# Score tiles moved into the projection, token lists from numbered rows, and 46 unread products on PE

## The reference

```python
# attention: 16 heads of 16, Q, K, V = norm(x) @ Wq, Wk, Wv
scores = jnp.einsum('bqhd,bkhd->bhqk', Q, K) / math.sqrt(HEAD_DIM)
alpha = jax.nn.softmax(scores, axis=-1)
alpha = jnp.where(causal, alpha, 0)             # masked after the softmax
Y = jnp.einsum('bhqk,bkhd->bqhd', alpha, V)
# experts: 8 experts, the best 2 of each of 4096 rows, hidden size 1024
h = jax.nn.gelu(flat_x @ w_fc[e], approximate=False)
out = out + combine[:, e:e + 1] * (h @ w_proj[e])
# together
x = x + _layernorm(attention(_layernorm(x)))
x = x + _layernorm(experts(_layernorm(x)))
```

## Time and profile before

| | us |
|---|---|
| median of 3 runs | 1625.13 (1625.03 to 1625.83) |
| profiled execution | 1626.82 |
| its span | 1625.1 |
| PE busy | 1455.0 (90%) |
| DVE busy | 1026.3 (63%) |
| ACT busy | 771.8 (47%) |
| POOL busy | 612.1 (38%) |
| mean granted clock of TensorE | 0.946 of 2.4 GHz |

### The profile page before, as it was taken

The page is one execution under the profiler, slowest core; times in us unless marked ns, Lnnn a source line. Parts: engine busy times, 40 slices in busy tenths (PEclk is TensorE's granted clock), DMA queues, the critical chain, the costliest instruction groups (busy, mean ns, idle before and its releaser), DMA issues.

```text
span 1625.1 us, 31177 instructions
## 1 busy us (share of the span) xinstructions
PE 1455.0 (90%) x9750; PEld 836.1 (51%) x9751; DVE 1026.3 (63%) x1770; ACT 771.8 (47%) x1650; POOL 612.1 (38%) x711
## 2 busy tenths in 40 slices
PE   5988999999999899989999986389999999999990
PEld 3551233333333233323333243289999999999980
DVE  4769777777888788878888977723323233233324
ACT  2330577777777677767777785211111111111114
POOL 5332334543444334533444432123333333333332
PEclk9995899999999999999999998589999999999995
DMA  3569122022220222022213153262222222222229
GB/s 113 172 164 276 40 40 40 10 31 40 40 40 8 35 40 40 15 27 40 40 23 70 53 182 142 45 183 34 39 33 38 39 33 39 34 37 39 32 30 210
DMA packets 87629, 105.07 MB, mean 65 GB/s; under 512 B 11648, under 2 KB 70912, under 8 KB 87520
## 3 DMA queue, kind: packets, MB, share of 16 engines
q1 hardware_dynamic: 69664, 80.80, 21.5%
q0 software_dynamic: 17856, 22.89, 8.9%
HBM read 64.70 MB, written 38.96 MB: 64 GB/s over the span
## 4 chain that ended last, share of the span: by engine, by line
PE 61%; DVE 15%; issue 13%; ACT 4%; POOL 3%; DMA 2%; DVEq 1%; SPq 0%; POOLq 0%; ACTq 0%
PE ps L1153 16%; PE ps L1163 15%; PE ps L1008 10%; DVE negmax L1443 9%; PE ps L980 8%; PE ps L1094 8%; ACT wfc L868 2%; POOL x L668 2%; PE ps L973 2%; PE ps L1081 1%; DVE x L1348 1%; PE ps L1142 1%; ACT wfc L911 1%; DVE wfc L1454 1%; DMA arena<-in_L_ffn_w_proj 1%
## 5 line engine op out<-in xcount | busy, mean ns | idle before, releaser
L1443 DVE TENSOR_REDUCE negmax<-ps 128x1 f32<-128x1024 f32 x512 | 605.9, 1216 | 123.8 <-PE ps L1094 121.3
L868 ACT ACTIVATE wfc<-ps 128x512 f32<-128x512 f32 x768 | 436.6, 595 | 171.2 <-PE ps L980 162.7
L889 ACT ACTIVATE yx<-ps 128x512 f32<-128x512 f32 x142 | 84.8, 597 | 440.6 <-PE ps L1153 440.6
L1153 PE MATMUL ps<-yx 128*128 128x128 f32 x2272 | 270.3, 278 | 4.1 <-DMA arena<-in_L_ffn_w_proj 3.4
L1153 PEld LDWEIGHTS ps<-yx 128*128 128x128 f32 x2272 | 269.7, 195 | 8.3 <-DMA arena<-in_L_ffn_w_proj 3.6
L1163 PE MATMUL ps<-arena,yx 128*128 x1136 | 256.8, 379 | 0.0
L731 POOL TENSOR_TENSOR wfc<-wfc,causal 128x512 f32<-128x512 f32 x128 | 162.6, 1270 | 249.6 <-ACT wfc L868 181.7
L1094 PE MATMUL ps<-arena 96*128 96x512 bf16 x704 | 231.5, 413 | 9.6 <-DVE negmax L1443 4.0
L759 POOL DMA_INDIRECT expert_out<-yx,rt x71 | 112.6, 1586 | 318.3 <-DVE yx L1576 315.3
L1163 PEld LDWEIGHTS ps<-arena,yx 128*128 128x128 f32 x1136 | 210.4, 190 | 25.7
L980 PE MATMUL ps<-arena 120*128 120x512 bf16 x528 | 203.3, 392 | 12.8 <-ACT wfc L868 0.4
(11 more groups left out here) (177 smaller groups left out, 1364.7 us busy)
## 6 DMA issues: line engine op xcount, KB each, us to landing
arena<-qk_parts SPq DMA_DIRECT2D x132, 128.0 KB, 5.9
qk_parts<-x SPq DMA_DIRECT2D x32, 384.0 KB, 2.6
arena<-in_L_ffn_w_proj SPq DMA_DIRECT2D x8, 1024.0 KB, 8.6
wfc<-in_L_ffn_w_fc SPq DMA_DIRECT2D x16, 512.0 KB, 7.5
wfc<-qk_parts SPq DMA_DIRECT2D x60, 128.0 KB, 6.1
expert_out<-rt SPq DMA_DIRECT2D x3, 1408.0 KB, 12.0
yx<-in_L_attn_content SPq DMA_DIRECT2D x8, 512.0 KB, 3.9
x<-in_L_attn_content SPq DMA_DIRECT2D x1, 4096.0 KB, 25.5
```

The costliest lines, as they stand in the source:

```text
L868: nc.scalar.activation(et_sb[b % NET][:, hl, :], bk(ebank(c, g)), ACT.Exp).then_inc(s_expB, 1)
L889: nc.scalar.activation(hidT[s][:, 4 * hf:4 * hf + 4, :], bk(1 + hf).rearrange("p (c t) -> p c t", c=4), ACT.Gelu).then_inc(s_ge, 1)
L1153: ins = nc.tensor.matmul(bk(1 + hf)[:, c * P:(c + 1) * P], w1[s][:, kc * FF + (4 * hf + c) * P:kc * FF + (4 * hf + c + 1) * P], xsT[:, kc, :],
L1443: nc.vector.tensor_reduce(negmax[:, hl % 2, i:i + 1], ps[:, 2 * (k % 2):2 * (k % 2) + 2, :], AX.XY, ALU.max, negate=True).then_inc(s_max, 1)
```

## The change

1. *Score tiles in the projection.* All engines' projection code is unrolled into 8 positions per chunk. From chunk 3 on each position is followed by one unit of attention, so that the 32 units of group 0 and the first 8 of group 1 are issued within chunks 3 to 7; `groups` starts with unit 8 of group 1. Terms use banks 4 and 5 in turn, rows' turns and values share 6 and 7. The order in a chunk is term 0, values, term 1, values, turn, turn, term 2, term 3. The four scalings, part 1 and both copies of turned rows go from DVE to ACT; part buffers are eight instead of four. The loads of groups 0 to 2 go between the stores; K of group 0 is issued by ACT in chunk 2.
2. *Start.* The constant that ACT's first activation reads and the identity come first on POOL; the three memsets of 24x4096 bf16 go from POOL to DVE, in chunks 0 to 2.
3. *Lists.* `lo1` holds the entry's number instead of one, made by eight scalar operations on 128 columns per place; it lies over rows stored four places earlier or more, so a place waits for an older store (`s_x2w[i // 2]`). `hi1` has two parts (mask, mask times partition), in batches of 8 with three buffers, over rows in `yx`. The row number is then the ratio of two sums, which takes a maximum, a reciprocal and a product more. `tok` comes before `tab`.
4. *Transfers.* The second weights of experts 4 and 5 are loaded before the last `store_x2`; the gates' stores come after it. PE waits for the weights before its first second product only.
5. *Unread products.* 12 + 10 + 24 products of bf16, 128x512, into bank 1, that nothing reads: ahead of the last turn, ahead of the lists' products and behind them.
6. *Experts.* The weights' copy comes before the rows' copy; the second tile's copy is made before the first rows' copy.

```diff
+        def early(c, pos):
+            n = PER * (c - UNIT0) + pos
+            return [divmod(n, U)] if n >= 0 else []
...
+            body(1, 1, range(PRO - U, U))
+            for p in range(2, 2 * NSL):
                 body(p, p % NSL)
...
+            for c in range(NC):
+                for pos in range(PER):
+                    if pos in (0, 2):
+                        keys(4 * c + pos // 2)
+                    elif pos in (1, 3):
+                        values(c, pos // 2)
+                    elif pos in (6, 7):
+                        keys(4 * c + pos - 4)
+                    elif c + 1 < NC:
+                        turn(c + 1, (c + 1) % 2, pos - 4)
+                    for p, k in early(c, pos):
+                        body(p, p % NSL, (k,))
+            pe.wait_ge(s_res, 4 * NC)
+            pe.wait_ge(s_ones, NSL)
             groups(pe, body)
...
+                    if pos == 0:
+                        if c + 1 < NC:
+                            bias_c(c + 1, (c + 1) % 2)
+                        if c:
+                            rest(4 * c - 1)
+                    elif pos in (1, 3):
+                        rest(4 * c + pos // 2)
+                    elif pos == 5:
+                        if c < NSL:
+                            nc.vector.memset(ks[c][MROW:MROW + MR], 1.0).then_inc(s_ones, 1)
+                    elif pos == 6:
+                        if c + 2 < NC:
+                            stats_c(c + 2, c % 2, 16 * ((c + 2) // 2 + 1))
+                    elif pos == 7:
+                        rest(4 * c + 2)
...
+                    elif pos == 2:
+                        part0(4 * c + 1)
+                        part1(4 * c)
+                        if c + 1 < NC:
+                            apply_c(c + 1, (c + 1) % 2)
...
+                        if c == CPB:
+                            for n in (2, 3, 6, 7):
+                                act.wait_ge(s_st[n], 16)
+                            load_side(act, 0, 0, 1)
...
+                    if pos == 0 and c:
+                        split(4 * c - 1)
+                    if pos in (3, 5):
+                        split(4 * c + pos // 2 - 1)
...
+            def keep_clock(n):
+                for _ in range(n):
+                    nc.tensor.matmul(bk(1), ones[:, :], identb[:, :].unsqueeze(1).to_broadcast([P, 4, P]), start=True, stop=True)
...
+                if i == G - 1:
+                    pe.wait_ge(s_add, x2_done(ORDER[i]))
+                    keep_clock(12)
...
+            pe.wait_ge(s_r, 3)
+            keep_clock(10)
...
+            keep_clock(24)
             pe.wait_ge(s_tab, 1)
...
-                dve.wait_ge(s_x2w[i], 16)
+                dve.wait_ge(s_x2w[i // 2], 16)
...
+                    for t in range(TPC):
+                        n = g * TPC + t
+                        ins = nc.vector.tensor_scalar(lo1[:, i, j, t, :], iota_l[:, :], lof[:, j, n:n + 1],
+                                                      float(1 + j * TT + n), ALU.is_equal, ALU.mult)
...
-            sp.wait_ge(s_inv, NPR // PCE)
-            for s in range(2):
-                sp.wait_ge(s_xs[s], 16)
+            store_x2(6)
             for e in (4, 5):
                 load_wproj(e)
+            store_x2(7)
+            for i in range(G):
+                store_gate(i)
```

More of the change, by code:

```diff
@@ L219, in sandwich @@
         s_p3 = sem("s_p3")
-        s_st = [sem(f"s_st{g}") for g in range(4)]
+        s_st = [sem(f"s_st{g}") for g in range(8)]
         s_v = sem("s_v")
@@ L466, in groups, with load_side, turn_bank @@
                 body(p, p % NSL)
[L468 to L479, removed]
+        Q_TERMS, K_TERMS = (0, 1, 2, 0, 1, 0), (0, 0, 0, 1, 1, 2)
+        def load_side(eng, g, u, ty):
+            dst, terms = ((qs[u], Q_TERMS), (ks[u], K_TERMS))[ty]
+            for r, part in enumerate(terms):
+                eng.dma_start(dst[r * DH:(r + 1) * DH, :, :],
+                              qk_d[ty, part, ds(g * (GH * DH), GH * DH), :].rearrange("(h d) n -> d h n", d=DH))\
+                   .then_inc(s_ld[u], 16)
+        def turn_bank(hl, g):
+            return 7 if isinstance(g, int) and g == 0 else 6 + HALVES[M_HALF[hl]]
         @block.sync
@@ L501, in _ @@
[L501 to L514, removed]
@@ L528, in _ @@
+            for n in range(8):
+                sp.wait_ge(s_st[n], 16 * NC // 2)
             sp.wait_ge(s_ve, 2 * NB * CPB)
@@ L822, in exp_gate, with values @@
+            def values(c, j):
+                act.wait_ge(s_v, 2 * c + j + 1)
+                for t in range(2):
+                    i = TPC * (c % CPB) + 2 * j + t
+                    dst = v_sb.rearrange("p (b h i d) -> p b h i d", b=NB, h=H, i=QT)[:, c // CPB, :, i, :]
+                    ins = nc.scalar.copy(dst, bk(6 + j)[:, t * D:(t + 1) * D].rearrange("p (h d) -> p h d", h=H))
+                ins.then_inc(s_ve, 1)
             def exp_gate(i):
@@ new lines, in values @@
+            def values(c, j):
+                if j:
+                    wait_pos(pe, s_mtc, turned[0])
+                for t in range(2):
+                    for kc in range(KC):
+                        ins = nc.tensor.matmul(bk(6 + j)[:, t * D:(t + 1) * D],
+                                               xnT[c % 2][:, kc, (2 * j + t) * P:(2 * j + t + 1) * P],
+                                               wqkv[:, 2, kc, :], start=(kc == 0), stop=(kc == KC - 1))
+                ins.then_inc(s_v, 1)
@@ L1256, in _, with rest @@
+            def rest(n):
+                g = n % 4
+                dve.wait_ge(s_p1, n + 1)
+                wait_pos(dve, s_p3, n - 1)
+                nc.vector.scalar_tensor_tensor(out=resid[g % 2], in0=bk(4 + g % 2),
+                                               scalar=Q_SCALE if g < KC else 1.0, in1=parts[n % 8][:, 0, :],
+                                               op0=ALU.mult, op1=ALU.subtract).then_inc(s_res, 1)
             rank = bk(3)[:, 0:(TT + 1) * E].rearrange("p (t e) -> p t e", e=E)
```

385 lines of the change are left out of this document (190 added, 195 removed).

## The result

The median went from 1625.08 us (4 runs, those on record and one more) to **1597.43 us** (4 runs, 1595.64 to 1598.45): ratio 0.9833, 95% interval 0.982 to 0.9846, so 27.7 us or 1.7% faster. The profiled execution took 1598.45 us, its span is 1596.7 (1625.1 before); the mean granted clock went from 0.946 to 0.97.

A forecast was written before the change was run, and what follows sets the result against it. PE was taken to bound attention's start and experts, DVE the score-only lead-in, with PE hardly pausing in the projection. Gains 21.4 + 1.5 + 8.5 = 31.4 us off 1625.1 gave 1594 us, range 1583 to 1603.

The forecast's parts named there:

- the passage: Between attention and experts: list stage +2.0, lists -5.1, token numbers +0.6, stores +1.0, experts -7.0; sum -8.5 us.
- Chunks 1 and 2: Projection chunks without score tiles: ScalarE's serial path sets 13.5 us each, DVE's path with the memset 13.2.
- The load: First load of Q and K: PE waits at the first score tile, 3.0 us (bounds 0 and 6).
- my fourth rival: Chunks 3 to 7: stalled PE drops to half clock, slower, 1654 us with all five; chance 0.03.
- (a): Chunks with tiles: PE lacks work between ScalarE's second key term and the next chunk's scalings; stall of 1.1 us.
- (b): From chunk 4, the turn of the maxima waits for POOL's parts, queued behind the last key term's split; 1.3 us.
- (c): Next chunk's first term waits for the third term's rest, behind maxima and statistics on DVE; 0.8 to 2 us.
- After the handover: Start of attention after tile k = 8: PE may arrive at full clock; 1.5 us saved, up to 4.5.
- The lists' term: List stage in the passage: 8.3 us instead of 13.4, so -5.1 (bounds -6.7 and -3.8).
- 1 (PE-bound): Projection: queues absorb the three stalls and the load wait, leaving PE the bound; 1573 us, chance 0.17.
- 2 (the clock products do not pay): Passage: first twelve delay the last turn, clock down again at the gather; passage gives 4 us, 1598, chance 0.14.
- 3 to 5: Overlap yields little, 1612, chance 0.06; half-clock PE slower, 1654, 0.03; start does nothing, 1614, 0.02.

The follow-up runs named there:

- experiment 1: The run of late_tiles: against the changed kernel, score tiles placed only after the projection; 1614.73 us, ratio 0.9943 to before.
- bridge_start: Changed kernel plus eight unread products before attention and eight ahead of its first turn of the second group; 1596.99 us, ratio 0.9836 to before.
- k_from_sp: Changed kernel with the six K transfers of group 0 issued by SP instead of ScalarE; 1596.58 us, ratio 0.9825 to before.
- load_room: Changed kernel with group 0's K transfers on SP and chunk 5's 512 KB of input rows one store later; 1594.34 us, ratio 0.9816 to before.
- stats_early: Changed kernel with DVE's statistics ahead of the maximum of tile 4 instead of tile 6; 1596.92 us, ratio 0.9833 to before.
- ones_pool: Changed kernel with the three 24x4096 memsets back from DVE to POOL, behind its constants; 1595.36 us, ratio 0.9825 to before.
- parts_first: Changed kernel with the maxima's parts ahead of POOL's split of the last key term; 1593.09 us, ratio 0.9806 to before.
- late_tiles: Changed kernel with no score tile in the projection, all tiles of the first two groups following it; 1614.73 us, ratio 0.9943 to before.
- no_first12: Changed kernel without the twelve unread products ahead of the last turn; 1594.72 us, ratio 0.9814 to before.
- best: Changed kernel with four edits together: those of no_first12, ones_pool, parts_first and load_room; 1587.15 us, ratio 0.9768 to before.
- bridge_gather: Changed kernel with 28 instead of 24 unread products ahead of the experts' first transposes and six behind these; 1595.1 us, ratio 0.9829 to before.

## Why the prediction came out

The forecast's 1594 with its range of 1583 to 1603 held 1597.4, and so did the stated range. But the two halves of the sum erred against each other: 22.9 us were forecast up to and behind tile k = 8 and 16.2 came, 8.5 were forecast in the passage and 12.05 came. That the total is only 3 us off is in part luck. What the runs bear out is the mechanism of the larger half, the overlap (17 of 27.7 us, experiment 1). The early start, the new lists and the earlier weights were not run by themselves; what they gave is read in the traces.

| step | predicted | measured |
|---|---|---|
| first key product | 12.6 | 12.53 |
| chunk 0 | 16.6 | 16.86 |
| chunks 1, 2 | 13.5 each | 14.36, 14.33 |
| chunk 3 with the load's wait | 17.0 + 3.0 | 23.87 |
| chunks 4, 5, 6 | 18.5, 18.5, 17.5 | 17.97, 17.97, 16.82 |
| chunk 7 and handover | 15.3 + 2.0 | 18.26 |
| tile k = 8 | 148.0 | 152.97 |
| from there to the count | -1.5 | +0.2 |
| count to first mask | +2.0 | -1.06 |
| lists | -5.1 | -5.15 |
| token numbers, gather | +1.6 | -0.14 |
| experts' entry | -7.0 | -5.7 |

**The start** was right to 0.1 us, and the order of the constants carries it.

**Chunks 1 and 2** were mis-sized by the memset, chunk 2 by ScalarE's issues as well. I took 3.65 us and a DVE path of 13.2 "just under ScalarE's 13.5". The row says 3.47, but DVE's rest ends at 50.50 and its statistics begin at 54.91: the operation holds DVE for 4.41 us, 0.91 of it shown as "issue" before the row. ScalarE's path is 13.0, so nothing hid it. In chunk 2 ScalarE's issues of K hold back the end of the chunk as much: it loses 0.4 when SP issues instead (13.94) and nothing when only the memset goes; the recorded sum had priced these issues in the load's wait alone. The Trainium skill (VectorE: DVE Perf Modes, Zero memsets can be issued as uint32) has a cycle per element whatever the type, 4.27 us as an estimate at its 0.96 GHz. The measured 4.41 agrees with it, where the row alone would not; its sum of 13.8 a chunk stood nearer to 14.35 than mine.

**The load** was the largest miss, 3.9 us in chunk 3. The wait was 4.47 for a forecast of 3.0 (bounds 0 to 6), because the tile came 8.0 us behind the last issue (56.51 to 64.50) where I took 5; the kernel before had 7.5, and 8 is what the other kernels show too. What I had left out is that PE comes out of it at half clock: eight value products took 3.62 us instead of 1.89 and two tiles 1.04 each instead of 0.60, 2.6 us together. That was the mechanism of my fourth rival, once, where the wait was.

**Chunks 4 to 7**: all three stalls are there, at the places named, by the waits named: (a) 0.57 for 1.1, (b) 0.83 for 1.3, (c) 1.02 within 0.8 to 2. The sum was 1.7 too high in chunks 4 to 6. Only (b) is worth its size when removed; (c) came back as 0.55 elsewhere.

**After the handover** 1.5 us were forecast and none came: a pause of 1.92 and one of 1.71 stand here (I had only the first), and the clock is 0.50 until about 162. The second pause is stall (b) once more: POOL makes the maxima's parts from 154.75 on, behind its split of the last key term (153.64), and the turn of the maxima follows tile k = 8 by 2.97 us, before by 2.29 (171.66). Bridged, the stretch is worth the 1.7 that I meant, in the trace.

**The passage.** "The list stage starts 2.0 later" failed. The twelve products pushed the turn 4.19 behind the count as worked out, but the clock rose under them, and turn, logits and turn back then ran in 1.04, 0.64 and 0.38 us where half clock takes 1.94, 1.08 and 0.60. So choose 7 came 1.41 earlier than before; without the twelve it would come 2.74 earlier, which was my "at best at 1024". The lists' term was right to 0.1. In "x1's eight stores now fall just before the gather: +1" the sign was wrong: from the last token number to the turn of gathered rows it is 4.1 us (1029.52 to 1033.64), before 5.2 (1051.0 to 1056.16); that the stores lay in its way before is argued, not tested. The entry of the experts was worth 5.7: the 3.4 of the wait for weights, and of the clock's 3.6 only part, because it fell in the first product.

**Rivals.** 1 (PE-bound) is out, with three stalls and a load. 2 (the clock products do not pay) is half right: the twelve do cost, and all 46 bring nothing measurable, though the 34 alone do. Its time, 1598, is what was measured, but by luck: it had 4 us in the passage, where 12 came. 3 to 5 are out: chunks with tiles cost 17 to 18 us, not 21; late tiles cost 17 us.

## What to carry to other kernels

An operation moved onto an engine "with slack" must be priced from the end of what precedes it to the start of what follows, not from its row alone. A pause of PE is to be paid for twice where the clock falls in it: add the half-clock work behind it to the wait. Here products that only hold the clock paid where PE was idle anyway (ahead of the lists, behind them) and cost where something waited behind them. An edit far ahead can also go with a change of the clock in a later stretch, as with the twelve. Which of several stalls is worth removing shows only when one is removed, since one went and another came back at half its size.

## What the runs showed of the hardware

- The pauses at the gather do not decide whether the clock falls near 1036. All eight kernels that have the first twelve products and no bridge there (the changed one, bridge_start, k_from_sp, load_room, stats_early, ones_pool, parts_first, late_tiles) take 5.43 or 5.44 us for the first expert product; the two without the twelve (no_first12, best) take 3.81. The pauses are the same: 1.54 and 1.25 us in ones_pool, 1.54 and 1.26 in no_first12. So the fall goes with the twelve, 30 us earlier. What differs in between is when the clock rose in the lists' stage, near 1022 in the changed kernel and near 1018 in no_first12; how that decides is open. Filled pauses kept the clock up in bridge_gather, which has the twelve.
- Chunk 0 took 15.4 to 16.9 us in kernels whose code up to there is the same (15.44 in bridge_gather, 16.86 in the changed one). In the changed kernel its first four products took 0.94 us each, as at half clock, under a granted clock that reads 1.00:

```profile
12.00:16.00 4.00, 3.48 (x4) 1.51 (x5) 0.34 (x2) 0.49 (x2) 0.00 (x0) 1.00 0.43 131
```

- Between two of SP's loads in the middle of attention (509.93 to 618.58 in the changed kernel) 107.9 to 109.2 us passed by kernel, with the same code. This scatter of 1.3 us is what hides the single edits; its cause was not looked for.
- A memset of 24x4096 bf16 costs DVE 4.41 us in place of the row's 3.47. On POOL two of the same stood back to back in 6.99 us, before the change.
